# Issuing a kernel's tile loads from ScalarE, between its copies, instead of from SyncE

## The reference

```
Kf  = einsum('bjd,ed->bje', F, K_w)
S   = einsum('bid,bjd->bij', F, Kf)
out = einsum('bij,ijd->bid', S, W) + einsum('bid,ed->bie', F, Q_w)
```

## Time and profile before

| | before |
|---|---|
| median of 3 runs | 612.51 us (611.63 to 613.41) |
| profiled execution, its own time | 613.91 us |
| its span | 612.1 us |
| TensorE busy | 599.2 us |
| ScalarE busy | 401.9 us |
| VectorE busy | 399.3 us |
| mean granted TensorE clock | 0.996 |
| DMA traffic | 137.60 MB, 225 GB/s on average |

### The profile page before, as it was taken

How to read it: one execution, slowest core, us unless ns; L and a number is a source line. 1 busy time by engine, 2 the same in 40 slices (tenths; PEclk the granted TensorE clock), 3 DMA queues, 4 the chain that set the end, 5 groups by cost and what they waited for, 6 DMA issues and landing times.

```text
span 612.1 us, 17936 instructions
## 1 busy us (share of the span) xinstructions
PE 599.2 (98%) x7694; PEld 529.0 (86%) x7694; DVE 399.3 (65%) x412; ACT 401.9 (66%) x698; POOL 0.2 (0%) x4
## 2 busy tenths in 40 slices
PE   9999999999999999999999999999999999999994
PEld 7888989888898888989889898898988889889894
DVE  6556768566594665947558575676856659466386
ACT  7978393864928659294692938849386492966920
POOL 0000000000000000000000000000000000000000
PEclk9999999999999999999999999999999999999998
DMA  8543956638475483764738556394663847558076
GB/s 320 239 169 123 339 199 248 236 147 320 155 276 209 181 304 137 286 233 196 256 134 332 220 212 247 123 335 190 263 221 149 320 153 276 209 183 301 0 277 276
DMA packets 29452, 137.60 MB, mean 225 GB/s; under 512 B 3264, under 2 KB 4032, under 8 KB 21312
## 3 DMA queue, kind: packets, MB, share of 16 engines
q1 hardware_dynamic: 28944, 136.20, 58.7%
q10 hardware_dynamic: 432, 0.26, 0.1%
HBM read 69.34 MB, written 67.11 MB: 223 GB/s over the span
## 4 chain that ended last, share of the span: by engine, by line
PE 97%; issue 1%; DVE 1%; DVEq 0%; ACT 0%; ACTq 0%
PE ps L488 20%; PE ps L433 20%; PE ps L435 19%; PE ps L434 19%; PE ps L514 18%; PE ps L537 1%; DVE o_sb L364 1%; DVEq L43 0%; DVE f_hi L378 0%; ACT s_t L298 0%; ACTq L43 0%; ACT s_t L296 0%; DVE o_sb L373 0%
## 5 line engine op out<-in xcount | busy, mean ns | idle before, releaser
L329 DVE TENSOR_TENSOR f_lo<-f_ring,f_hi 128x1024 fp32r<-128x1024 f32 x124 | 151.8, 1224 | 171.3 <-ACT f_hi L221 169.7
L235 ACT ACTIVATE q_out<-ps 128x512 f32<-128x512 f32 x256 | 157.1, 614 | 6.7 <-PE ps L435 0.2
L364 DVE TENSOR_TENSOR o_sb<-ps,q_out 128x1024 f32<-128x1024 f32 x127 | 145.2, 1216 | 20.7 <-PE ps L514 20.7
L226 ACT ACTIVATE kf<-ps 128x512 f32<-128x512 f32 x256 | 155.9, 609 | 3.3
L244 ACT ACTIVATE s_t<-ps 128x512 f32<-128x512 f32 x32 | 19.1, 598 | 181.2 <-PE ps L488 181.2
L488 PE MATMUL ps<-f_ring,kf 128*64 128x64 f32 x4096 | 126.3, 223 | 3.0 <-issue 3.0
L488 PEld LDWEIGHTS ps<-f_ring,kf 128*64 128x64 f32 x4096 | 122.8, 138 | 6.4 <-issue 4.6
L514 PEld LDWEIGHTS ps<-s_t,w_sb 64*128 64x128 f32 x2048 | 115.6, 188 | 6.7 <-issue 5.3
L514 PE MATMUL ps<-s_t,w_sb 64*128 64x128 f32 x2048 | 118.6, 274 | 1.3 <-ACT s_t L298 1.3
L433 PE MATMUL ps<-f_hi,k_hi 128*128 128x512 f32 (+1 forms) x258 | 101.9, 395 | 0.0
L435 PE MATMUL ps<-f_hi,k_lo 128*128 128x512 f32 (+1 forms) x258 | 100.4, 389 | 0.0
(11 more groups left out here) (30 smaller groups left out, 158.1 us busy)
## 6 DMA issues: line engine op xcount, KB each, us to landing
out<-o_sb SPq DMA_DIRECT2D x127, 512.0 KB, 3.5
f_ring<-f_t SPq DMA_DIRECT2D x62, 1024.0 KB, 4.8
w_sb<-w SPq DMA_DIRECT2D x1, 2048.0 KB, 19.1
f_ring<-f SPq DMA_DIRECT2D x6, 256.0 KB, 5.1
out<-o_sb SPq DMA_DIRECT2D x2, 256.0 KB, 2.2
f_ring<-f SPq DMA_DIRECT2D x3, 128.0 KB, 2.6
f_ring<-f ACTq DMA_DIRECT2D x1, 128.0 KB, 2.8
s_t<-k_t ACTq DMA_DIRECT2D x1, 64.0 KB, 2.5
```

The costliest lines, as they stand in the source:

```text
L226: nc.scalar.activation(kf[:, c // 2, c % 2 * CK:(c % 2 + 1) * CK, :, :].rearrange("d k h i -> d (k h i)"), ps[:, 2 * c % 8, :], COPY).then ...
L235: nc.scalar.activation(q_out[:, t % 2, :, :].rearrange("d i (h b) -> d i h b", h=2)[:, :, :, at:at + CK], ps[:, (2 * c + 1) % 8, :].rearra ...
L329: nc.vector.tensor_tensor(f_lo[:, v % SPLIT, :], f_unit(v), f_hi[:, v % SPLIT, :].bitcast(F32), ALU.subtract).then_inc(flo_done, 1)
L364: nc.vector.tensor_tensor(o_sb[:, n % OBUF, :, :], ps[:, bank:bank + 2, :], q_out[:, t % 2, :, :].rearrange("d (s m) b -> d s (m b)", s=2) ...
```

## The change

SyncE's function `load_next` and its calls are gone, so its queue carries the first loads, W and then stores alone. ScalarE gets a function of the same name, called after the second `copy_s` of a tile and after `copy_q` of chunks 3, 7 and 11. The 58 loads concerned, their sizes and their targets are the same. The wait on `k_done` is left out; the wait on `s_done` stays, and its value is 2j+2 for load 0 also, where it was 7.

```diff
-            def load_next(t, j):
-                p = t * PAIRS + j + RING
-                if p < TILES * PAIRS:
-                    if j == 0:
-                        sp.wait_ge(s_done, t * UNITS + 7)
-                    else:
-                        sp.wait_ge(s_done, t * UNITS + 2 * j + 2)
-                        sp.wait_ge(k_done, (t + 1) * CHUNKS + 4 * j - 2)
-                    load_f(p)
...
-                for j in range(PAIRS):
-                    load_next(t, j)
...
+            def load_next(t, j):
+                p = t * PAIRS + j + RING
+                if p < TILES * PAIRS:
+                    act.wait_ge(s_done, t * UNITS + 2 * j + 2)
+                    act.dma_start(f_ring[:, p % RING, :, :, :, :].rearrange("d u k h i -> d (u k h i)"),
+                                  f_t[p, :, :]).then_inc(f_in[p % RING], 16)
...
             for t in range(1, TILES):
                 copy_s(t - 1, 1)
                 copy_s(t - 1, 3)
+                load_next(t - 1, 0)
                 for c in range(CHUNKS):
                     copy_kf(t, c)
                     copy_q(t, c)
+                    if c in (3, 7, 11):
+                        load_next(t - 1, c // 4 + 1)
```

## The result

| | before | after |
|---|---|---|
| median | 612.35 us (4 runs, 611.63 to 613.41) | 608.23 us (4 runs, 607.87 to 609.50) |
| profiled execution, its own time | 613.91 us | 607.87 us |
| its span | 612.1 us | 606.1 us |
| TensorE busy | 599.2 us | 596.1 us |

What follows compares the result with a forecast made beforehand. The prediction took TensorE as the bound. Removed SyncE issues, added ScalarE issues and moved load times each counted 0, so the profiled 613.91 us stayed and the median was forecast at 612.5 us, range 609.5 to 615.6.

Steps and rivals of the forecast that it cites:

- The pause: TensorE's scores, after the 146th matmul: a stop that makes a tile 0.64 us longer, in nine tiles.
- Rival 1: Scores: the pause becomes rarer as loads leave the stores' queue; all nine gone saves 5.8 us, giving 606.7; chance 0.12.
- in the window of the pause only stores run, before as after: Argument against Rival 1: load 0 follows the pause and load 3 has landed by the rows.
- The term set at 0: The loads' moved issue times: every landing stays hidden from the work that needs its data, so 0 us.
- A landing would have to take 2.2 us longer: Loads: landing takes 4.7 to 4.8 us from issue; only 2.2 us more, in every tile, would be felt.
- The two casts: VectorE's casts of units 4 and 6, after loads 0 and 1: each expected 0.6 us later, hidden.
- x = 0.33: ScalarE's projections: one load issue costs the engine 0.33 us, 19 us over 58 issues, covered by its slack.
- The split of chunk 5: ScalarE's projections: this split starts 0.33 us late, at 231.68, after two added issues, without delaying TensorE.
- The point x = 0.60: ScalarE's cost per issue from which the late last Q copy delays sums and scores, so that TensorE waits.
- rival 3: ScalarE: an issue holds it longer than 0.60 us; at 0.74 TensorE loses 7.8 us, giving 620.3; chance 0.07.
- The queue: Rival 1's mechanism: with the loads off the stores' queue, TensorE's instruction fetch could meet another order there.

Runs made afterwards that it cites:

- e4: The kernel before with 20 more always-met waits on TensorE in tile 2 alone, which came to 8 instructions: 609.75 us in its one execution.
- e6: The kernel before with load 1 alone issued at its later time (3.5 us later), still by SyncE: 607.78 us, no pause.
- e11: The changed kernel plus an unneeded 1 MB write by SyncE at 17.4 us after the rows' start, 15 times in all: 611.74 us.
- e13: The changed kernel plus an unneeded 1 MB write at 17.4 us after the rows' start in every second tile, 7 in all: four pauses; time not stated.
- e14: The changed kernel plus an unneeded 1 MB write in every tile at about 28 us after the rows' start: 607.69 us, no pause.
- e12: The changed kernel with each of ScalarE's 58 loads cut in four of 256 KB, issued one behind the other: 611.01 us.
- e1: The kernel before, loads still issued by SyncE but at the times they have in the changed kernel: 607.79 us, no pause.
- e9: The kernel before with load 1 waiting for the third chunk's K product instead of the second's (issued at 18.7 us): no pause; time not stated.
- e10: The kernel before with load 1 waiting for the fourth chunk's K product (about 20.1 us): as expected, none or one pause; measured time not stated.

## Why the prediction was wrong

- **The bound, TensorE, and its one repeated wait: right.** The pause was seen, sized (0.64 us in nine tiles) and named as the only place where time could be saved. Rival 1, with all nine gone, gave 5.8 us less than the median; the spans differ by 6.0. It had a chance of 0.12, and its price was right because it counted the nine pauses; its mechanism was another (below). The range missed by 1.3 us: four pauses and the scatter add up to 3.5 us, which would have given 609.0, still above 608.23.
- **The step that failed is the argument against rival 1**: "in the window of the pause only stores run, before as after". True, and not the question. It looked at the traffic beside the pause; the traffic that decides runs a tile earlier, near 18 us after the rows' start. In all profiles but e4, one stage in 85 pauses (by 0.34 us or more) when block 4 before it starts by 20 us, 4 in 19 between 20 and 21, and 56 in 106 from 21 on; what shows the cause is e6, e11, e13 and e14, where one large transfer at 17.4 us was taken away, put back, put back in every second tile and put elsewhere. The same step moved all four loads and asked of each only who waits for its data. It never asked who else uses the DMA engines at the old and the new moment: load 1 made way for TensorE's own instructions. The term set at 0 was worth 6.0 us in the profiled pair, 4.1 in the medians.
- **"A landing would have to take 2.2 us longer" and nothing late from the loads: right**, and with more room than forecast. I put the issues at 224.3, 229.4, 234.5 and 239.6, that is 17.5, 22.7, 27.8 and 32.8 us after the rows' start. That tile has a pause of 0.64 us; without it they are 16.9, 22.0, 27.1 and 32.2. They came at 15.1, 20.8, 26.2 and 31.6, since the sequencer reaches them ahead of the copies. From load 1 on they are 5.44 us apart, TensorE's pace for four chunks, where I had taken 5.1. Landings stayed at 4.8 us. The two casts did not move.
- **x = 0.33: too high, it is 0.** The split of chunk 5 is not 0.33 us later; it starts 9.0 us after the first projection, as before. The Trainium skill ("Perfetto Trace Analysis", on the DMA instruction by HWDGE) has the sequencer held for the recorded length. e12 agrees, where four in a row stop the copies for 0.9 us; that the copies stop for a single one does not follow from it, and the trace after shows that they don't.
- **The point x = 0.60: the chain behind it was wrong.** I let the first sum of a tile wait for the Q copies just made. `q_copied >= (t + 1) * CHUNKS` for the sums of tile t counts tile t's own copies, and those in question are of tile t+1. In e12 the last Q copy ends at 1.47 us and the first sum still starts at 1.21. What waits for that copy is row block 3, near 2.8 us. It changed no number of the forecast, only the price of rival 3.
- **The queue**: that the loads reach the pause through the stores' queue was the picture in rival 1 ("the fetch could meet another order there"). e1, with no pause and the loads on that queue, shows that the queue isn't needed.

Still open: how a large transfer at 17.4 us, or the late block 4 behind it, makes block 2 of the next tile 1 us later. Block 1, between them, starts at 1.0 to 1.6 us in either case, and only about half the late ones have the effect. In e4, where the borders lie 8 instructions elsewhere, the pauses follow an early block 4 and go with a block 1 that starts after the rows' start. That fits a part played by block 1, and was not tested.

## What to carry to other kernels

A moved transfer is to be checked against everything that uses the DMA engines at its old and at its new time, the engines' instruction fetches too, and its effect may come a stage or a tile later. When TensorE waits on "issue" always at the same matmul, add a few instructions ahead: if the pause moves by as many, it is instruction supply, and then the times of large transfers are what to vary. Count them in the profile, since 20 waits here were 8 instructions. Here one wait on SyncE (load 1 on a later chunk, e6) gives all that the change gives, with nothing on ScalarE.

## What the runs showed of the hardware

- TensorE's instruction blocks share the DMA engines with data: 16.4 KB each, and 2.4 us late (21.9 instead of 19.5) behind 1 MB in flight.
- A load's first packet starts about 0.97 us after its issue (e9, e10).
- TensorE's next block began its transfer some 2.8 us before the first matmul behind the border (8.8 and about 11.6 us after the rows' start, undisturbed tiles). Its transfer had ended at least 1.3 us before that matmul in every undisturbed stage.
- ScalarE's sequencer runs ahead of its copies, 0.9 us at load 1 (issue at 189.04, the next copy at 189.97): one DMA issue of 0.33 us is free, four in a row stop them for 0.9 us there (e12). Issues right behind another cost 0.45 us instead of 0.33.
- The issue of a tile's last store takes 1.4 us in paused tiles and 0.4 to 0.6 us in others (before), though nothing waits for it: a sign on SyncE of when the instruction block fell among the stores.
